# A chunked gated delta rule of 16 heads: its triangular systems inverted in 32x32 diagonal blocks on VectorE and GpSimd and solved by halves

## The reference, cut to what matters

```python
q = x @ w_q; k = x @ w_k; v = x @ w_v
beta = sigmoid(x @ w_b) * 2.0
g = -exp(A_log) * softplus(x @ w_a + dt_bias)
q, k, v = (_causal_conv_silu(t, conv) for each)   # 4 taps over time, per channel
q = _l2norm(q); k = _l2norm(k)
def step(S, inp):                                  # one token after the other
    S = S * exp(g_t)[..., None, None]
    mem = einsum('bhk,bhkv->bhv', k_t, S)
    delta = (v_t - mem) * b_t[..., None]
    S = S + einsum('bhk,bhv->bhkv', k_t, delta)
    o_t = einsum('bhk,bhkv->bhv', q_t * scale, S)
rms = o * rsqrt(mean(o * o) + EPS)
y = rms * norm_w * silu(x @ w_g)
return y @ w_out
```

## Time and profile before

| | us |
|---|---|
| three runs | 8037.87, 8038.21, 8055.04 (median 8038.21) |
| the profiled execution | 8059.97 |
| its span | 8057.8 |
| mean granted TensorE clock | 0.91 of full speed |

### The profile page before, as it was taken

How to read it: one execution, slowest core, us unless ns; L and a number is a source line. 1 busy time by engine, 2 the same in 40 slices (tenths; PEclk the granted TensorE clock), 3 DMA queues, 4 the chain that set the end, 5 groups by cost and what they waited for, 6 DMA issues and landing times. The chain is left out here.

```text
span 8057.8 us, 129070 instructions
## 1 busy us (share of the span) xinstructions
PE 6848.8 (85%) x45278; PEld 4941.3 (61%) x45278; DVE 4460.4 (55%) x13472; ACT 2489.6 (31%) x5229; POOL 1371.5 (17%) x1447
## 2 busy tenths in 40 slices
PE   6769969999999999999999997899879789500289
PEld 3538857777777777777777775787556444200254
DVE  8666654555555555555555554666568541399620
ACT  2323322333333333333333332233257222300132
...
GB/s 20 4 29 16 16 68 0 0 0 0 0 0 0 0 0 0 0 0 0 0 0 0 0 0 23 17 16 20 0 3 0 10 15 0 73 0 0 21 15 10
DMA packets 24078, 75.60 MB, mean 9 GB/s; under 512 B 1816, under 2 KB 15912, under 8 KB 21808
## 3 DMA queue, kind: packets, MB, share of 16 engines
...
## 5 line engine op out<-in xcount | busy, mean ns | idle before, releaser
L1474 PEld LDWEIGHTS l1a_m_bank<-l1a_m_W,l1a_m_Y 128*128 128x128 f32 (+1 forms) x6144 | 731.2, 183 | 329.0 <-DVE l1a_m_W L1835 218.3
L1835 DVE TENSOR_TENSOR l1a_m_W<-l1a_m_bank,const 128x256 f32<-128x256 f32 x768 | 326.1, 425 | 1061.1 <-PE l1a_m_bank L1464 1061.1
L1637 ACT COPY l1a_m_Y<-l1a_m_bank 128x512 f32<-128x512 f32 x768 | 450.0, 586 | 1212.1 <-PE l1a_m_bank L1454 1194.2
L1464 PEld LDWEIGHTS l1a_m_bank<-l1a_m_X,l1a_m_NT 128*128 128x128 f32 (+1 forms) x6144 | 694.5, 183 | 112.6 <-issue 111.6
L1474 PE MATMUL l1a_m_bank<-l1a_m_W,l1a_m_Y 128*128 128x64 f32 (+1 forms) x6144 | 743.2, 264 | 11.4 <-DVE l1a_m_W L1835 1.9
L1464 PE MATMUL l1a_m_bank<-l1a_m_X,l1a_m_NT 128*128 128x64 f32 (+1 forms) x6144 | 741.7, 264 | 0.8 <-ACT l1a_m_X L1633 0.8
L1842 DVE TENSOR_TENSOR l1a_m_X<-l1a_m_X,l1a_m_bank 128x256 f32<-128x256 f32 (+1 forms) x768 | 324.1, 422 | 522.7 <-PE l1a_m_bank L1474 514.3
L1406 PE MATMUL l1a_m_bank<-l1a_folded,l1a_m_xpad 128*128 (+1 forms) x1024 | 556.9, 626 | 0.7 <-ACT l1a_m_fade L1625 0.7
L1396 PE MATMUL l1a_m_bank<-l1a_folded,l1a_m_xpad 128*128 (+1 forms) x1024 | 519.2, 610 | 6.2 <-POOL l1a_m_xpad L1702 2.2
L3062 PE MATMUL l3a_h_mix<-l3a_w,l3a_h_oT 128*128 128x128 f32 x64 | 16.5, 440 | 572.9 <-DMA l3a_h_oT<-l3a_o 563.8
L1454 PEld LDWEIGHTS l1a_m_bank<-const,l1a_m_X 128*128 128x128 f32 x3072 | 356.8, 141 | 219.2 <-DVE l1a_m_X L1842 193.3
...
## 6 DMA issues: line engine op xcount, KB each, us to landing
...
```

Of the source, the lines that this page charges most:

```text
L1464: last = nc.tensor.matmul(bank[u][0][live(k), hh * HALF:(hh + 1) * HALF], NT[u][:, hh, live(k)], left(X[u][:, hh, :], k), start=True, stop ...
L1474: last = nc.tensor.matmul(bank[u][1][live(k), hh * HALF:(hh + 1) * HALF], Y[u][:, hh, live(k)], W[u][:, hh, :], start=True, stop=True)
L1637: nc.scalar.copy(flat(Y[u]), bank[u][2][:, :]).then_inc(Y_saved[u], 1)
L1835: nc.vector.tensor_tensor(W[u][:, :, :], bank[u][0][:, 0:HG * HALF].rearrange("p (h t) -> p h t", h=HG), g.c("level")[:, k * HALF:(k + 1) ...
```

## The change

The main stage is written anew. The constants of the six levels go, and the weight tiles change: only v's taps are folded.

- q and k are projected channel-major, once for both tiles of a unit (256 tokens), four products in all. ScalarE writes the last tap, VectorE adds the other three in six instructions per half (`convolve`). Squares are summed by a product with a selector, and turned; lengths go into the factors of beta, of v and of the final mean square in place of scaling q and k.
- Of every triangle only the four 32x32 diagonal blocks are inverted. SyncE stores them to DRAM (four transfers a tile), and loads the 64 blocks of two groups (two tiles, four heads, four blocks each) with one block per partition. Forward elimination then runs over rows: VectorE takes columns 0 to 11, GpSimd the others (`L1A_SPLIT = 12`), each with a product and an addition per row. ScalarE turns the result, SyncE stores both forms and loads them back by tile (`load_xd`, five transfers).
- TensorE joins two 32x32 inverses to one of 64x64 (`couple`, `join`), and solves a tile by halves: `solve_upper`, `cross` (upper result into the lower half), `solve_lower`.
- The read of the state is subtracted in four instructions of VectorE from PSUM; `read_state` puts its products into two banks.
- The transposed input is written to DRAM once (2 MB) and read per batch by SyncE.
- The order has one slot per group: a prepares group i of a batch, c4 finishes group i of the batch before, c3 starts the next group's first tile, e is an elimination, in slots 0 and 2. All loops are over batches, with 4 slots ahead and 4 behind: 68 slots.
- VectorE's order in a slot is: subtract the read (c4), convolve a's first half, rows 1-2, mean square (c4, tile 0), rows 3-4, silu of v (c3), add the cross product (c4), rows 5-7, convolve the second half, norm, lower delta (c4), rows 8-10, silu of q, k and gate, rows 11-12, output, rows 13-14, lengths, keys, rows 15-17, add the read, dots of a's first tile, rows 18-21, mean square (tile 1), rows 22-24, silu of v and cross product (c3), rows 25-30, norm, dots of the second tile, lower delta and gate (c3), output. GpSimd's rows lie between its own steps in the same manner. Rows are there only in slots 0 and 2.

The diff, cut to its core:

```diff
-def turn_X(u, n, k):
-  pe.wait_ge(merged[u], n * LEVELS + k)
-  for hh in range(HG):
-    last = nc.tensor.transpose(bank[u][2][:, hh * P:(hh + 1) * P], X[u][:, hh, :], g.c("ident"))
-  last.then_inc(X_turned[u], 1)
-def products_NX(u, n, k):
-  if k == 0:
-    pe.wait_ge(mixT_begun[u], n + 1)
-    pe.wait_ge(X_ready[u], n + 1)
-  for hh in range(HG):
-    last = nc.tensor.matmul(bank[u][0][live(k), hh * HALF:(hh + 1) * HALF], NT[u][:, hh, live(k)],
-                left(X[u][:, hh, :], k), start=True, stop=True)
-  last.then_inc(W_ready[u], 1)
-def products_XW(u, n, k):
-  if k > 0:
-    pe.wait_ge(Y_saved[u], n * LEVELS + k)
-  pe.wait_ge(W_masked[u], n * LEVELS + k + 1)
-  for hh in range(HG):
-    last = nc.tensor.matmul(bank[u][1][live(k), hh * HALF:(hh + 1) * HALF], Y[u][:, hh, live(k)],
-                W[u][:, hh, :], start=True, stop=True)
-  last.then_inc(XW_ready[u], 1)
...
-def mask_W(u, n, k):
-  dve.wait_ge(W_ready[u], n * LEVELS + k + 1)
-  nc.vector.tensor_tensor(W[u][:, :, :], bank[u][0][:, 0:HG * HALF].rearrange("p (h t) -> p h t", h=HG),
-              g.c("level")[:, k * HALF:(k + 1) * HALF].unsqueeze(1).broadcast_to([P, HG, HALF]),
-              ALU.mult).then_inc(W_masked[u], 1)
-def merge(u, n, k):
-  x = left(flat(X[u]), k)[live(k), :, :]
-  dve.wait_ge(XW_ready[u], n * LEVELS + k + 1)
-  nc.vector.tensor_tensor(x, x, bank[u][1][live(k), 0:HG * HALF].rearrange("p (i s) -> p i s", s=2 << k),
-              ALU.subtract).then_inc(merged[u], 1)
...
+def slots(bb, begin=False, end=False):
+  for i in range(NG):
+    a = None if end else (bb, i)
+    c4 = None if begin else (bb - 1, i)
+    c3 = (bb - 1, i + 1) if i < NG - 1 else (bb, 0)
+    if (begin and i < NG - 1) or (end and i == NG - 1):
+      c3 = None
+    e = (bb - 1, 1) if i == 0 else (bb, 0) if i == 2 else None
+    if (begin and i == 0) or (end and i == 2):
+      e = None
+    slot(a, c4, c3, e, i)
...
+def store_n(a, u):
+  b, i = a
+  sp.wait_ge(nT_ready, tiles(a, u))
+  for q in range(4):
+    sp.dma_start(n_d[i // 2, (i % 2) * TPB + u, :, q, :, :].rearrange("h j i -> j h i"),
+          nT[i][u][block(q), :, block(q)]).then_inc(n_stored, 16)
+def load_n(a):
+  b, i = a
+  sp.wait_ge(n_stored, (num(a) + 1) * TPB * 4 * 16)
+  sp.dma_start(en[:, :, :].rearrange("n j i -> n (j i)"),
+        n_d[i // 2].rearrange("t h q j i -> (t h q) (j i)")).then_inc(n_loaded, 16)
...
+sp.wait_ge(x_stored, (c[0] * SETS + i // 2 + 1) * 32)
+sp.sem_inc(sp_begun, 1)
+free(sp, lower_ready, tiles(c, u) - 2)
+sp.dma_start(Xd[u][:, :, :], x_d[at[0], at[1]].rearrange("h q i c -> (q i) h c")).then_inc(xd_loaded[u], 16)
+for q in range(4):
+  sp.dma_start(Y1[u][block(q), :, block(q % 2)],
+        y_d[at[0], at[1], :, q, :, :].rearrange("h c i -> c h i")).then_inc(xd_loaded[u], 16)
...
+for r in range(2):
+  for k in range(2):
+    last = nc.tensor.matmul(pa[r][:, k * N:(k + 1) * N], wqk[:, i, r, k, :],
+                xa[:, bass.ds(b & 1, 1), :], start=True, stop=True)
+  last.then_inc(qk_projected, 1)
...
+def couple(c, u):
+  b, i = c
+  pe.wait_ge(xd_loaded[u], (num(c) + 1) * LOADS)
+  free(pe, lower_delta, tiles(c, u) - 1)
+  begin()
   for hh in range(HG):
+    for e in range(2):
+      last = nc.tensor.matmul(bs[block(2 * e + 1), hh * B32:(hh + 1) * B32],
+                  nT[i][u][block(2 * e), hh, block(2 * e + 1)], Xd[u][block(2 * e), hh, :],
+                  start=True, stop=True)
+  last.then_inc(W_ready, 1)
...
+def solve_upper(c, u):
+  pe.wait_ge(V_saved, tiles(c, u))
+  if u == 0:
+    pe.wait_ge(rhs_ready, tiles(c, u))
+  else:
+    pe.wait_ge(read_subtracted, num(c) + 2)
+  begin()
   for hh in range(HG):
+    last = nc.tensor.matmul(bs[upper, hh * DV:(hh + 1) * DV], Y1[u][upper, hh, :], R[u][upper, hh, :],
+                start=True, stop=True)
+  last.then_inc(upper_ready, 1)
+def cross(c, u):
+  pe.wait_ge(upper_saved, tiles(c, u))
+  begin()
   for hh in range(HG):
+    last = nc.tensor.matmul(bs[lower, hh * DV:(hh + 1) * DV], nT[c[1]][u][upper, hh, lower], Dl[u][upper, hh, :],
+                start=True, stop=True)
+  last.then_inc(cross_ready, 1)
+def solve_lower(c, u):
+  pe.wait_ge(cross_added, tiles(c, u))
+  begin()
   for hh in range(HG):
+    last = nc.tensor.matmul(bs[lower, hh * DV:(hh + 1) * DV], Y1[u][lower, hh, :], R[u][lower, hh, :],
                 start=True, stop=True)
+  last.then_inc(lower_ready, 1)
...
+def slot(a, c4, c3, e, i):
+  if c4 is not None:
+    new_state(c4)
+    couple(c4, 1)
+    mix(c4, 0)
+  if a is not None:
+    project_qk(a)
+  if c4 is not None:
+    join(c4, 1)
+    read_state(c4)
+  if c3 is not None:
+    project_v(c3, 0, (0, 1))
+  if c4 is not None:
+    solve_upper(c4, 1)
+  if c3 is not None:
+    project_v(c3, 0, (2, 3))
+  if c4 is not None:
+    cross(c4, 1)
+  if a is not None:
+    decays(a, 0)
+  if c4 is not None:
+    solve_lower(c4, 1)
+  if c3 is not None:
+    project_gate(c3, 0)
+  if c4 is not None:
+    turn_y(c4, 0)
+  if a is not None:
+    sum_squares(a)
+  if c4 is not None:
+    project_out(c4, 0)
+  if a is not None:
+    turn_sums(a)
+    turn_k(a)
+  if c3 is not None:
+    couple(c3, 0)
+  if c4 is not None:
+    mix(c4, 1)
+  if a is not None:
+    decays(a, 1)
+  if c3 is not None:
+    join(c3, 0)
+  if a is not None:
+    dots(a, 0)
+  if c3 is not None:
+    project_v(c3, 1, (0, 1))
+    solve_upper(c3, 0)
+    project_v(c3, 1, (2, 3))
+    cross(c3, 0)
+  if a is not None:
+    dots(a, 1)
+  if c3 is not None:
+    solve_lower(c3, 0)
+    project_gate(c3, 1)
+  if c4 is not None:
+    turn_y(c4, 1)
+    project_out(c4, 1)
...
+def eliminate(e, rows):
+  S = L1A_SPLIT
+  for j in rows:
+    low, n = B32 - 1 - j, j - S
+    old, new = ex[:, j + 1:B32, S:j], tmp_p[:, 0:low, 0:n]
+    if j > S + 1:
+      pool.wait_ge(ep_step, 2 * (j - S - 1))
+    nc.gpsimd.tensor_tensor(new, en[:, j, j + 1:B32].unsqueeze(2).broadcast_to([BLOCKS, low, n]),
+                ex[:, j, S:j].unsqueeze(1).broadcast_to([BLOCKS, low, n]),
+                ALU.mult).then_inc(ep_step, 1)
+    pool.wait_ge(ep_step, 2 * (j - S) - 1)
+    nc.gpsimd.tensor_tensor(old, old, new, ALU.add).then_inc(ep_step, 1)
...
+def convolve(a, r):
+  b, i = a
+  dve.wait_ge(tap_saved, num(a) * 2 + r + 1)
+  for d in range(1, PAD + 1):
+    for k in range(2):
+      n = 2 * (d - 1) + k
+      if d > 1:
+        dve.wait_ge(conv_step, num(a) * CONV + r * (CONV // 2) + n - 1)
+      nc.vector.scalar_tensor_tensor(acc[:, r, k, d:N], pa[r][:, k * N:(k + 1) * N - d],
+            taps[:, i, r, k, PAD - d:PAD - d + 1], acc[:, r, k, d:N],
+            ALU.mult, ALU.add).then_inc(conv_step, 1)
...
+def eliminate(e, rows):
+  for j in rows:
+    low, n = B32 - 1 - j, min(j, L1A_SPLIT)
+    old, new = ex[:, j + 1:B32, 0:n], tmp_v[:, 0:low, 0:n]
+    if j == 1:
+      dve.wait_ge(ex_begun, sets(e) + 1)
+    else:
+      dve.wait_ge(ev_step, 2 * (j - 1))
+    nc.vector.tensor_tensor(new, en[:, j, j + 1:B32].unsqueeze(2).broadcast_to([BLOCKS, low, n]),
+                ex[:, j, 0:n].unsqueeze(1).broadcast_to([BLOCKS, low, n]),
+                ALU.mult).then_inc(ev_step, 1)
+    dve.wait_ge(ev_step, 2 * j - 1)
+    nc.vector.tensor_tensor(old, old, new, ALU.add).then_inc(ev_step, 1)
...
```

More of the change, by code:

```diff
@@ L1208, in l1_attn @@
             summed = sp_.sem("summed")
+            spilled = sp_.sem("spilled")
             def each(a):
@@ new lines, in block, with run @@
+            def block(q):
+                return slice(B32 * q, B32 * (q + 1))
+            lower, upper = slice(P // 2, P), slice(0, P // 2)
+            def run(engine, first, slot):
+                def slots(bb, begin=False, end=False):
[9 more added lines that the diff above has]
+                        slot(a, c4, c3, e, i)
+                first()
+                slots(0, begin=True)
+                with engine.Fori(0, BATCH - 1) as it:
+                    slots(it + 1)
+                slots(BATCH, end=True)
@@ new lines, in new_state, with read_state @@
+                        last.then_inc(state_ready, 1)
+                    def read_state(c):
+                        b, i = c
+                        pe.wait_ge(state_saved, num(c) + 1)
+                        pe.wait_ge(gate_silu, tiles(c, 1))
+                        begin()
+                        for swap in range(2):
+                            if swap:
+                                pe.wait_ge(read_begun, num(c) + 1)
+                                begin()
+                            for r in range(2):
+                                for k in range(2):
+                                    hh = 2 * r + (k + swap) % 2
+                                    last = nc.tensor.matmul((bt if k == 0 else bg)[:, hh * DV:(hh + 1) * DV],
+                                                            qkT[i][half_rows(hh), r, k, P:2 * P], state[half_rows(hh), r, :],
+                                                            start=True, stop=True)
```

(23 more changed lines are left out.)

1224 lines of the change are left out of this document (680 added, 544 removed).

## The result

| | before | after |
|---|---|---|
| runs | 8037.87 to 8055.04, four, median 8045.94 | 7679.02, 7685.76, 7692.25, 7698.71, median 7689.01 |
| profiled execution, span | 8059.97, 8057.8 | 7679.02, 7677.2 |
| mean granted TensorE clock | 0.91 | 0.817 |

The ratio is 0.9556, 95% interval 0.9537 to 0.9575: faster by 357 us. The forecast was 7480, so 558 faster than the median then shown: the sign and the range were right, and the time came out 209 us above the forecast.

A forecast was written before the change was run, and what follows sets the result against it. TensorE, busy 99% of the main stage, was taken as the bound. Stage -540, load -11 and folding -8 took the profiled 8059.97 to 7501, and 7480 since that execution stood 22 above the median; range 7000 to 7900.

The forecast's parts named there:

- TensorE's 35 us per group: Main stage: TensorE's work per group falls from 58.0 to 35 us; open prices of small products move it 31 to 42.
- The group without elimination, 42: Main stage: TensorE's 35 us, about 4 of waits and 3 for a lower clock make 42 us.
- the sum, 30 x (58 + 42): Main stage: 30 long and 30 short groups, 3000 us, plus 235 make 3235 for 3775.5: -540.
- The group with elimination, 58: Main stage: 10 us until VectorE has subtracted and convolved, then 48 of mutually excluding work: 58 us.
- What excludes each other is 18.9 + 2.6 of VectorE and 27 of GpSimd: Group with elimination: VectorE's and GpSimd's SBUF instructions exclude each other whole, so their times add to 48 us.
- the rival with dear short instructions (1.0): GpSimd's 36 elimination instructions cost 1.0 us, not 0.31; long group grows by 25 us, time 8254; chance 0.06.
- VectorE's rows: Elimination on VectorE, columns 0 to 11: 60 instructions, 7640 elements in all, 18.9 us.
- DRAM: Elimination blocks' way through DRAM: landings 2.2 us and up to twice that, largely covered by VectorE's first 10 us.
- the second: Rival on TensorE: small tiles cost 0.27 and clock is low; groups take 50 and 62, time 7859; chance 0.15.
- The first, no exclusion of consequence: Rival: short VectorE and GpSimd instructions slip between each other; long group 44 to 45, time 7069; chance 0.17.
- the 235 forecast: Main stage's edges: four first places with only preparation and four last with only solving, 231 taken as 235 us.
- Load and folding: Before the main stage: a smaller load gives -11 us, halved folding of taps -8.

The follow-up runs named there:

- e10: Changed kernel with last rows at place's end, TensorE's loop in 3 passes, earlier batch load, v products ahead, all 31 elimination columns on VectorE: 7197.8 us.
- e6: Changed kernel with TensorE's loop in 3 passes of 5 batches and the next batch's transposed input loaded two places earlier: 7603.1 us.
- e3: Changed kernel with TensorE's loop over 15 batches written as 3 passes of 5, same instructions and order: 7660.1 us.
- e2: Changed kernel with all 31 elimination columns on VectorE and none on GpSimd: 7681.1 us.
- e1: Changed kernel without the elimination's row instructions on VectorE and GpSimd, result not the reference's: 7146.8 us, one run.
- e4: Changed kernel with only VectorE's written order changed, convolutions and first-tile steps ahead of the first elimination rows: 7693.2 us.
- e9: Changed kernel with 12 unread products of 512 columns added in TensorE's waits of each long slot: 7571.8 us.

## Why the prediction was right, and where it was off

- **The bound and the change's direction**: right. TensorE was the whole stage before, and what it was relieved of came off the period until other things held.
- **TensorE's 35 us per group**: 3.4 too much, within its bounds of 31 to 42. With the same 237 records it is busy 36.0 at a clock of 0.88 and 31.6 at 1.00 (e10), and the 35 were priced at full clock. The open prices: eight products of 32x32 start 0.37 us before the next group, so 0.05 each where I took 0.11; four of 64x64 take 1.01, so 0.25 where I took 0.23. The rows, start and duration:
```profile
2888.39 0.44 PE L1619 MATMUL l1a_m_bs<-l1a_m_Xd,l1a_m_nT 32*32 32x32 f32 x16
2888.76 1.16 PE L1722 MATMUL l1a_m_bm<-l1a_m_Dl,l1a_m_mixT 128*128 128x128 f32 x8
...
2898.31 1.08 PE L1650 MATMUL l1a_m_bs<-l1a_m_Dl,l1a_m_nT 64*64 64x128 f32 x8
2899.32 1.12 PE L1574 MATMUL l1a_m_px<-l1a_m_terms,const 128*128 128x512 f32 x2
```
- **The group without elimination, 42**: 42.5, made as forecast of TensorE's work, waits and clock, but by luck in the size: 31.6, 6.3 and 4.4 us in place of 35, 4 and 3. And only every second one. The other ends a loop pass.
- **The step that failed is the sum, 30 x (58 + 42)**: it had no term for the loop's end. It costs 7.1 to 7.2 us (e6), 14 times: 101 us, half of the 205 us by which the stage missed its forecast. In the kernel before, the end of a pass showed nothing, so I took the new loop, four slots long, as free too, and never asked what a pass of 4 x 237 = 948 TensorE records in place of 393 would do. The Trainium skill, Runtime: NRT & Kernel Launch, section Instruction fetch mechanics, says that a taken branch to code outside the fetched pages stalls the engine until its page has come, as prefetch is only sequential. The trace agrees: beside the 3.20 and 1.03 us at TensorE stand two loads of instructions of 16 KB, at every loop end, and e3 and e6 moved the idle time with the loop's end.
- **The group with elimination, 58**: 59.6 to 59.9, nearly the number, by luck, for a reason that fell. "What excludes each other is 18.9 + 2.6 of VectorE and 27 of GpSimd": e2 took 12 us off GpSimd and nothing happened. Only 5.8 us per elimination are exclusion of VectorE's rows. What fills the slot is VectorE's own list, 43 us busy with 23.2 of rows in it, in series with some 14 us of waits for TensorE (6.4 for the read at the slot's end, 7.4 inside the list; e1, e4), whose steps ran partly at 1.2 GHz (e9). Two errors met: exclusion much too dear, and VectorE's waits inside its list (output, dots, keys: 7.4 us) and the clock left out.
- **The page on the lock**: the Trainium skill, SBUF — State Buffer, section Who interferes with whom, says that a VectorE instruction with two SBUF inputs contends with a GpSimd one that reads SBUF, and calls contention an exclusive lock. The words "for the whole instruction" stand there for VectorE's two-port modes, and the prediction took them for this case too. The trace agrees for GpSimd's instructions of 512 elements alone: a row held by one shows the full stop (0.34 to 1.03), while rows of both engines side by side show 0.05 each, and rows beside the 1.01 us power of four columns 0.02. The measurement decides; why the power doesn't hold a row is open.
- **GpSimd's rows**: forecast about 0.31, measured 0.39 on average for the sums (one of the nine, beside VectorE's silu of q and k, takes 0.94) and 0.31 for the products, so the rival with dear short instructions (1.0) was wrong. Its power of eight columns took 1.64, in the forecast's bounds. First triangle 1.94, in 1 to 5.
- **VectorE's rows**: 18.9 forecast (its own terms add up to 18.7), 17.4 bare, 23.2 in fact. Two more slips of the sums change nothing: the high prices of the small products give TensorE 41 us and not 42, and GpSimd's short instructions would decide from 0.83 us and not from 0.87.
- **DRAM**: stores landed in 1.5 us, loads in 3.9, the forecast's 2.2 and up to twice that; the first triangle was done at 2893.37 and VectorE's subtraction began at 2893.70. Covered, as forecast.
- **Rivals**: the second had 50 and 62 for the two groups. Its small tiles were wrong, its clock right: TensorE was busy 41 us in a long slot with records that take 31.6 at full clock (e10), and e9 brought 3.5 of these 9.4 back to the period. The first, no exclusion of consequence, was right in that short instructions slip between each other (0.05 us each) and wrong in its price: it had the long group at 44 to 45, as it too let VectorE's list run without waits.
- **The sum by parts**: forecast -540 for the stage, measured 3440 - 3775 = -335. The 205 between them: loop ends 14 x 7.2 = 101, long slots 30 x 1.77 = 53, short ones 30 x 0.46 less 1.7 for the last of them = 12, and the edges 39 more than the 235 forecast (3440 less the 3166 of 60 slots = 274). Load and folding: from the first record of this step's statistics to the main stage: 83.2 to 65.5 us, -18 for the forecast's -19. The other 28 us lie in code that the change doesn't touch (16 ahead, 12 behind); among the twelve experiments that code behind the stage took 3063 to 3080 us, before 3076 and after 3064, so those 12 are within scatter. The 16 ahead are not wholly: this step began 1124 us into the span before, and 1107 to 1116 in the changed kernel and the experiments.
